# A new order of the stages on all four compute engines, and unread identity products of TensorE in its waits in the first five and last four tiles

## The reference, cut to what matters

```python
mod = (silu(L0_c) @ L0_wmod).reshape(2, 6, 1, 256)      # sa, ca, ga, sb, cb, gb
h = layernorm(x) * (1 + ca) + sa                         # x: (2, 4096, 256)
x = x + ga * attn(h)                                     # two RWKV layers, l = 0 and 1
h = layernorm(x) * (1 + cb) + sb
x = x + gb * ffn(h)                                      # three fp4-quantized products, 256 -> 704 -> 256

# one layer of attn:
x = x + time_mix(ln(x))      # tanh(xxx @ tm_w1), five mixes, r, k, v, g, decay w, then
#   out_t = r_t . (state + u * k_t v_t) ; state = state * w_t + k_t v_t  ; norm by head, * g, @ Wo
x = x + channel_mix(ln(x))   # sigmoid(r_in @ cWr) * (relu(k_in @ cWk)**2 @ cWv)
```

## Time and profile before

| | |
|---|---|
| time, three runs | 3195.91 us median, 3187.82 to 3196.2 |
| the profiled execution | 3192.44 us, span 3190.7 us |
| PE busy | 2926.2 us, 92% of the span |
| DVE busy | 2383.7 us, 75% |
| ACT busy, POOL busy | 1252.3 us (39%), 1270.3 us (40%) |
| mean granted clock of PE | 0.969 |
| DMA | 41.56 MB, mean 13 GB/s |

### The profile page before, as it was taken

The page is one execution under the profiler, slowest core; times in us unless marked ns, Lnnn a source line. Parts: engine busy times, 40 slices in busy tenths (PEclk is TensorE's granted clock), DMA queues, the critical chain, the costliest instruction groups (busy, mean ns, idle before and its releaser), DMA issues.

```text
span 3190.7 us, 79561 instructions
## 1 busy us (share of the span) xinstructions
PE 2926.2 (92%) x33341; PEld 2317.9 (73%) x33341; DVE 2383.7 (75%) x5345; ACT 1252.3 (39%) x2451; POOL 1270.3 (40%) x1456
## 2 busy tenths in 40 slices
...
PEclk7689999999999999999999999999999999999987
...
DMA packets 36313, 41.56 MB, mean 13 GB/s; under 512 B 2748, under 2 KB 34680, under 8 KB 35960
## 3 DMA queue, kind: packets, MB, share of 16 engines
...
...
## 4 chain that ended last, share of the span: by engine, by line
PE 67%; DVE 13%; issue 11%; POOL 7%; ACT 2%; DMA 0%; DVEq 0%; ACTq 0%; POOLq 0%
PE ps_all L1087 11%; PE ps_all L1309 10%; PE ps_all L1095 7%; PE ps_all L1276 6%; PE ps_all L1290 6%; PE ps_all L1199 6%; PE ps_all L1328 5%; PE ps_all L1079 3%; PE ps_all L1126 2%; DVE sxrk L954 2%; POOL grstd L605 2%; DVE att L961 2%; PE ps_all L1320 2%; PE ps_all L1173 1%; POOL sxrk L568 1%
## 5 line engine op out<-in xcount | busy, mean ns | idle before, releaser
L581 POOL TENSOR_TENSOR mixin<-mixin,hT_tm 128x512 f32<-128x512 f32 x320 | 375.6, 1179 | 912.4 <-DVE mixin L920 910.3
L954 DVE TENSOR_TENSOR sxrk<-sxrk,dec 128x512 f32<-128x512 f32 x384 | 301.7, 786 | 217.0 <-PE ps_all L1199 214.4
L1276 PE MATMUL ps_all<-chan,cwk 128*128 128x256 f32 x1536 | 362.7, 386 | 3.0 <-DVE ffn_work L1015 3.0
L1290 PE MATMUL ps_all<-cwv,chan 128*128 128x256 f32 x1536 | 348.6, 383 | 0.0
L1199 PEld LDWEIGHTS ps_all<-sxrk 64*64 64x64 f32 x12288 | 223.0, 137 | 158.6 <-issue 158.4
L1199 PE MATMUL ps_all<-sxrk 64*64 64x32 f32 x12288 | 259.2, 223 | 72.0 <-DVE att L961 68.3
L1290 PEld LDWEIGHTS ps_all<-cwv,chan 128*128 128x128 f32 x1536 | 286.5, 190 | 41.7 <-DVE ffn_work L1015 1.0
L1276 PEld LDWEIGHTS ps_all<-chan,cwk 128*128 128x128 f32 x1536 | 284.7, 190 | 42.7 <-DVE ffn_work L1015 3.8
L920 DVE SCALAR_TENSOR_TENSOR mixin<-ps_all,vcol,sxrk 128x256 f32<-128x256 f32 x640 | 272.4, 476 | 25.6 <-PE ps_all L1130 14.6
L563 POOL TENSOR_TENSOR rstd<-var,powc 128x2 f32<-128x2 f32 x224 | 179.8, 803 | 201.5 <-DVE var L867 192.0
L961 DVE COPY_PREDICATED att<-masks,ps_all 128x256 f32<-128x256 uint8 x384 | 201.5, 525 | 9.3
...
## 6 DMA issues: line engine op xcount, KB each, us to landing
...
```

Source lines behind the costliest of these rows:

```text
L581: pool.tensor_tensor(m, m, hT["tm", l][:, :, :, 1:P + 1].rearrange("p k c t -> p (k c) t"), ALU.add).then_inc(ev["mixed"][b], 1)
L954: v.tensor_tensor(rko, rko, t, ALU.mult).then_inc(ev["rk_lev"][b], 1)
L1276: ins = pe.matmul(bank(b, "ck", lj, "k")[:, m * TT:(m + 1) * TT], cwk[:, l, k, n:n + P], k_in[:, k, :], start=(k == 0), stop=(k == KC - 1))
L1290: ins = pe.matmul(bank(b, "cv", l, "v")[:, c * D:(c + 1) * D], relu[t // 2][:, t % 2, c * P:(c + 1) * P], cwv[:, l, t, :], start=(t == 0), ...
```

## The change

The table `ORDER` is new for all four engines: the same stages with the same work, in another sequence, so that the stages of the five streams are interleaved differently. Since banks 6 and 7 are given out in the order of PE's round, their uses move too. The diff shows the first line of the table of each kind.

```diff
 ORDER = {
-    PE: """1/3 ov.0; 0/1 pw1; 1/3 ov.1 st.1; 2/2 cv; 1/3 yt; 0/1 pk pr; 1/3 wo; 4/4 xt; 0/1 mf.4 mf.2; 4/4 gu.0.0; 0/1 pw2
...
+    PE: """1/2 pv; 4/4 ht.1; 1/2 lev.2; 4/4 dn; 2/1 turn.cm; 1/2 lev.3 pg lev.4; 0/0 turn.tm; 2/1 ck.0 ck.1; 1/2 lev.5; 2/1
...
+WAITING = {
+    0: """0 turn.tm 16; 0 mix 9; 0 mf.0 4; 0 pw1 7; 0 pk 2; 0 pr 3; 0 lev.3 4; 0 lev.5 5; 0 lev.6 3; 0 kt 2; 0 yt 11; 0 wo
+        7; 2 turn.cm 23; 2 ck.0 1; 2 cv 1; 1 turn.tm 3; 1 mf.0 2; 1 pw1 4; 1 lev.5 4; 1 lev.6 3; 1 kt 3; 1 yt 3; 1 wo 1;
+        3 ck.0 3; 4 xt 3; 4 ht.0 3; 4 ht.1 3; 4 dn 1""",
...
+    2: """0 mix 3; 0 pw1 13; 0 lev.3 3; 0 lev.5 1; 0 kt 3; 0 yt 10; 0 wo 1; 2 turn.cm 13; 1 turn.tm 1; 1 mix 2; 1 pw1 3; 1
+        pr 3; 1 lev.5 4; 1 lev.6 3; 1 kt 3; 1 yt 3; 1 wo 1; 3 turn.cm 1""",
+    3: """0 mix 3; 0 pw1 13; 0 lev.3 3; 0 lev.5 1; 0 kt 3; 0 wo 1; 2 turn.cm 13; 1 turn.tm 1; 1 mix 2""",
+    4: """0 mix 3; 0 pw1 13""",
...
+    -1: """0 lev.5 1; 0 kt 3; 0 wo 1; 2 turn.cm 13; 2 ck.0 3; 1 turn.tm 7; 1 mix 2; 1 mf.0 4; 1 pw1 3; 1 pr 3; 1 lev.3 13;
+        1 lev.5 5; 1 lev.6 4; 1 kt 2; 1 yt 12; 1 wo 2; 3 turn.cm 8; 3 ck.0 7; 3 cv 2; 4 xt 57; 4 gu.0.0 3; 4 ht.0 23; 4
+        ht.1 23; 4 dn 3""",
 }
...
-        def turns(eng, run, steps, meanwhile):
+        def turns(eng, run, steps, meanwhile, before=None):
 
             for i, b, kind, arg in run:
+                if before:
+                    before(i, b, kind, arg)
                 steps[kind](i, b, arg)
...
                 elif at == (0, "1 lna.tm"):
                     weights_grid(2)
+                    v.wait_ge(suq["q_out"], 3)
...
+            def unread(i, b, kind, arg):
+
+                name = stage_name(kind, arg)
+                n = count[i, b, name] if (i, b, name) in count else 0
+                if n:
+                    kind, arg, use = use_of[b, RESULT[name] if name in RESULT else name]
+                    fill(pe, i, b, kind, arg, use)
+                    for _ in range(n):
+                        pe.matmul(bank(b, kind, arg, use)[:, 0:P], ident[:, :], ident[:, :], start=True, stop=True)
...
-            turns(pe, RUN[PE], steps, meanwhile)
+            turns(pe, RUN[PE], steps, meanwhile, unread)
```

More of the change, by code:

```diff
@@ L26 @@
 ORDER = {
-    PE: """1/3 ov.0; 0/1 pw1; 1/3 ov.1 st.1; 2/2 cv; 1/3 yt; 0/1 pk pr; 1/3 wo; 4/4 xt; 0/1 mf.4 mf.2; 4/4 gu.0.0; 0/1 pw2
-        lev.1 pv; 3/3 turn.cm; 0/1 lev.2; 4/4 gu.0.1; 1/2 turn.tm; 0/1 lev.3 pg; 3/3 ck.0; 0/1 lev.4; 3/3 ck.1 ck.2 cr; 0/1
-        lev.5; 1/2 mix; 4/4 ht.0; 0/1 lev.6; 4/4 gu.1.0; 0/1 kt; 1/2 mf.0 mf.1 mf.3; 0/1 st.0 ov.0; 4/4 gu.1.1; 0/1 ov.1
-        st.1; 3/3 cv; 1/2 pw1; 0/1 yt; 1/2 pk pr; 0/1 wo; 1/2 mf.4 mf.2; 4/4 ht.1; 1/2 pw2; 4/4 dn; 1/2 lev.1 pv lev.2; 2/1
-        turn.cm; 0/0 turn.tm; 1/2 lev.3 pg lev.4; 2/1 ck.0 ck.1; 1/2 lev.5; 2/1 ck.2; 0/0 mix; 1/2 lev.6; 0/0 mf.0 mf.1
-        mf.3; 1/2 kt; 2/1 cr; 1/2 st.0""",
@@ L39 @@
[L39 to L45 removed]
+    PE: """1/2 pv; 4/4 ht.1; 1/2 lev.2; 4/4 dn; 2/1 turn.cm; 1/2 lev.3 pg lev.4; 0/0 turn.tm; 2/1 ck.0 ck.1; 1/2 lev.5; 2/1
+        ck.2; 0/0 mix; 1/2 lev.6; 2/1 cr; 1/2 kt; 0/0 mf.0 mf.1 mf.3; 1/2 st.0 ov.0 ov.1 st.1; 2/1 cv; 0/0 pw1 pk; 1/2 yt;
+        0/0 pr; 4/3 xt; 0/0 mf.4 mf.2; 1/2 wo; 0/0 pw2; 4/3 gu.0.0; 0/0 lev.1; 1/1 turn.tm; 0/0 pv lev.2; 3/2 turn.cm; 4/3
+        gu.0.1; 1/1 mix; 0/0 lev.3 pg; 3/2 ck.0; 0/0 lev.4; 1/1 mf.0 mf.1 mf.3; 0/0 lev.5; 3/2 ck.1 ck.2; 1/1 pw1; 0/0
+        lev.6; 1/1 pk; 0/0 kt; 3/2 cr; 1/1 pr; 4/3 ht.0; 1/1 mf.4 mf.2; 0/0 st.0 ov.0 ov.1 st.1; 4/3 gu.1.0 gu.1.1; 1/1 pw2;
+        0/0 yt; 3/2 cv; 1/1 lev.1; 0/0 wo""",
```

41 lines of the change are left out of this document (28 added, 13 removed), and 2 rows, old and new, of the table WAITING.

## The result

The changed kernel takes 3169.7 us (median of 4, 3167.6 to 3170.6); the kernel before takes 3195.1 us in the same comparison. The ratio is 0.9924, 95% interval 0.9907 to 0.9941. It is faster by 25 us, where 76 were forecast; 3169.7 lies in the range, 50 us above the forecast. The profiled execution took 3170.09 us, its span is 3168.3. The medians of the experiments are of undisturbed executions; one execution of lnb_first (7314 us) and one of before_abs (3465 us) ran far slower and are in no median and no ratio.

The account below looks back on a forecast made before the run. PE was taken to bound the middle, with only its idle time to save. Terms -57 - 6 - 33 + 20 = -76 us took the profiled 3192.44 to 3116.4, forecast 3120 us as median; 8-in-10 range 3068 to 3182.

Parts of the forecast that it names:

- steady order, 27 rounds: Middle rounds: the new order cuts PE's idle time from 3.87 to 1.8 us a round, 57 us in all.
- order at both ends, third matrix in it: Start: the third matrix's absolute value on ACT directly follows the exponentials, shortening DVE's 8.24 us wait; 6 us once.
- clock: Start and end: products keep PE working so its clock stays up; 22 and 11, together 33 us (bounds 0 and 57).
- products not hidden: Start and end: 20 us of the products' 159 us fall outside waits and are paid (bounds 0 and 70).
- unit price: One product on PE: 0.24 us, bounds 0.15 (a transpose) and 0.47 (half clock).
- halved work: PE work at half clock, 78 us at start, 37 at end: half, 39 and 18, is the most full clock returns.
- waits that were to go: Steady rounds, PE: 0.98 before `lev.1`, 1.45 in `lev.2` and `lev.3`, 0.58 before `pw2`, 0.28 before `yt` would vanish.
- what I could not see: Steady rounds: allowance of 0.5 us a round added to 1.3 us of remaining and new PE waits.
- Rival 2: Small gain in the middle, 0.7 us a round, because DVE comes late; about 3162 us, within 3140 to 3186; chance 0.18.
- Rival 3: Products do not hold the clock, all else as forecast; the 33 us are missing, 3153 us; chance 0.07.
- Rival 4: Slower: late DVE holds `gu.0.0`'s gate half, PE waits for bank 6; 3215 us at 3.5 more a round; chance 0.08.
- The sign of a first store later than 391 us: Start: a first store after 391 us would show the forecast wrong, meaning the products pushed PE.

Follow-up runs that it names:

- lnb_first: last_only with DVE's `lnb.cm` of stream 3 moved ahead of `lev.1` of stream 0; 3113.0 us, 0.9744 of the kernel before.
- before_abs: Kernel before with only `weights_abs(2)` on ACT moved behind the exponentials of the second round; 3184.0 us, 0.9983 of the kernel before.
- no_products: Changed kernel with the table of products empty, the new order alone; 3131.2 us, 0.9802 of the kernel before.
- last_only: Changed kernel with only the 109 products ahead of stream 4's stages in the last tile; 3120.1 us, 0.9771 of the kernel before.
- tile0_only: Changed kernel with only the 134 products of tile 0; 3132.1 us, 0.9825 of the kernel before.
- both_serial: last_only with the edits of pg_first and lnb_first and 61 more products in tile 0; 3116.4 us, 0.9776 of the kernel before.
- pg_first: last_only with PE's `pg` of stream 0 moved ahead of `turn.cm` of stream 3; 3098.6 us, 0.9704 of the kernel before.
- tiles1_4: Changed kernel with only the 232 products of tiles 1 to 4; 3155.0 us, 0.9875 of the kernel before.

## Why the forecast was right in direction and wrong in size

The ledger, in us. The measured column is of profiled executions, from stores and spans: the first two terms from no_products against before, the next two from the kernel after against no_products.

| term | forecast | measured |
|---|---|---|
| steady order, 27 rounds | -57 | -44.5 |
| order at both ends, third matrix in it | -6 | -18.4 |
| clock | -33 | } +40.5 together |
| products not hidden | +20 | } |
| sum | -76 | -22.4 |

1. **The step that failed is the clock with the price of its products.** The forecast said that 33 us come back and 20 of 159 are paid: -13. The kernel after against no_products measures +40.5 by the spans (3168.3 and 3127.8), 53.5 us the other way. The unit price was right at full clock, 0.24 against 0.235; at half clock a product took 0.48. Wrong was to set the 88 us of 366 products against the 94.3 us of idle time at the start: a sum over 400 us says nothing of whether each product lies in a wait of its size. Of the 88 us that PE is idle there in no_products, 75 lie in the first 200, and the products of tiles 2 to 4 stand where PE had some 13 us idle in 200. Nor had I asked what each wait is for: where it is for the bank that the product needs too, the product comes behind it (the 6.06 us at 44.83). By the experiments, in time up to tile 27's store: tile 0's +9.3, tiles 1 to 4 +31.1 when alone, both together in the kernel after +34.5. Behind it: +6.0, of which the 109 products of the last stream 4 give -8.0 in their interval; so the other 186 (43.7 us of PE) cost some 14 to 20 (19.6 by last_only against after). Those 186, in tiles 28 to 30 and in the other streams of the last tile, were never run by themselves; that figure is a remainder. How the +40.5 splits into clock won and products paid was not measured either.
2. **Half of "halved work" was not on the path.** I turned time at half clock into a gain by halving PE's work and taking 22 of 39 and 11 of 18 us. In the last tile, where PE's `gu` and `dn` are the chain, 8.0 us came, close to 11. In the first tile no gain shows: tile0_only lifts the clock of 30 to 100 us from 0.68 to 0.85 and stores tile 0 6.2 us later, both_serial lifts it without paying and wins 1.8, no more than such a store scatters. PE in order of time at the start, in no_products and then in the kernel after:

```profile
27.48 0.63 PE L1105 MATMUL ps_all<-ident,mixin 128*128 128x128 f32 x4 [0.93 <-DVE mixin L887]
31.41 2.05 PE L1137 MATMUL ps_all<-mixin,tm_w 128*128 128x256 f32 x4 [3.30 <-DVE mixin L911]
```

```profile
27.47 3.73 PE L1116 MATMUL ps_all<-ident 128*128 128x128 f32 x32
31.04 0.60 PE L1122 MATMUL ps_all<-ident,mixin 128*128 128x128 f32 x4
```

   PE's transposes take 0.6 us and then it waits 3.30 us for DVE: a faster PE would shorten little in such a stretch. And the first 16 products begin at 27.47, just when the tile is there whose wait they should bridge (27.48 in no_products); they take 3.73 us and push the transposes, and all behind them, 3.6 us back. How the 22 would split further was not tried.
   The sentence of the Trainium skill, page "TensorE: Matmul & The Clock Gate", Part 1, is that the ramp penalty is below 1% of a typical span. What the products of the last tile gave back here is 8 of 3128 us, 0.3%, although the time at half clock is 196 us or 6%. That is in line with it, but what the low clock costs in all no run shows, since none had the full clock at the start without added work. I had the sentence in the prediction and did not let it weigh on the sum.
3. **The steady order was right in its mechanism and 12 us too large.** All waits that were to go are gone. The residue of 2.14 us a round (58.6 us in 2500) was forecast at 1.8: `turn.cm` waits 0.90 for 0.4, because `lnb.cm` takes 1.42 us and not 0.70, and the scaling ahead of it 0.89 and not 0.69; the levels of stream 0 wait 0.6 together for 0.5; `ov.1` 0.34 for 0.4; `dn`, unforeseen, 0.28 (within the 0.5 for what I could not see). The idle time of a round came down by 1.73 us where 2.1 were forecast, 9 us of the 12. The round itself came down by 1.6, so some 0.1 of the saved idle time came back as something else; what was not tried. pg_first confirms the mechanism of the largest: one stage of 1.9 us ahead of `turn.cm` takes the wait away and 0.92 us off the round.
4. **The third matrix** was about right: DVE's wait is 2.53 instead of 8.24, 5.7 less, and 5.1 at tile 0's store when moved alone, for 6. But the order at the ends brought 12 more that I had at nothing: 14.2 before tile 0's store, of which about 5 are the matrix, and 4.2 behind tile 27's. PE's `turn.tm` of tile 1 starts at 101.9 us in no_products and at 105.1 before, of tile 2 at 192.8 and 202.3. This share was not taken apart further.
5. **The rivals.** Rival 2 gave 3162 for the wrong reason: it put the loss into the middle. Rival 3, that the clock would not hold, is refuted. Rival 4's wait is real (0.90 us against the 0.4), 0.5 more where 2.8 decide. The sign of a first store later than 391 us, for products that push PE, was the right test and caught it: 402.1.

The whole gain of no_products (-62.9) is the forecast's -63 for the order and the third matrix, but with two errors of 12 us that cancel; that agreement is luck.

Left open: the interval of tile 30 (the last but one) is 66.9 us in no_products and 63.1 to 65.4 in last_only, tile0_only and tiles1_4, which have no product there but the first of last_only's, 2.3 us before its end. The granted clock of that interval is 0.80 in no_products and 0.84 in tiles1_4 and tile0_only. So the longest interval has the lowest clock, and up to 4 us at the end go with it; why the clock differs there was not found. Differences of that size at the ends are not to be trusted from one profile.
